# Attention on one Trainium2 core: mixing moved to four quadrants in the logits' banks, the final in its own bank, normalising over two rounds

## The reference

```
n = 56*56 tokens, 8 images, 8 heads of 16
q, k, v = x @ Wq.T, x @ Wk.T, 2 * (x @ Wv.T)       # [n, 8, 16]
v_h = v / |v|;  q = q / |q|;  k = k / |k|
A = softmax(v_h @ v_h.T)                            # 8 x 8 per token
q, k = A @ q, A @ k                                 # mixing over heads
P = softmax(k.T @ q)                                # 16 x 16 per token
out = v @ P                                         # 8 x 16 per token
out = transpose(out, (0, 3, 1, 2)).reshape(n, 128)  # per image, across tokens
return out @ proj_w.T + proj_b                      # added to x
```

## Time and profile before

| | |
|---|---|
| median of 3 runs | 3337.49 us (3333.54 to 3340.35) |
| the profiled execution | 3327.52 us, span 3325.7 us |
| PE busy | 2987.1 us (90%), 62,769 matmul and 62,769 load instructions |
| DVE busy | 1866.8 us (56%) |
| ACT busy | 1275.8 us (38%) |
| POOL busy | 570.3 us (17%) |

### The profile page before, as it was taken

The page is one execution under the profiler, slowest core; times in us unless marked ns, Lnnn a source line. Parts: engine busy times, 40 slices in busy tenths (PEclk is TensorE's granted clock), DMA queues, the critical chain, the costliest instruction groups (busy, mean ns, idle before and its releaser), DMA issues. The chain is left out here.

```text
span 3325.7 us, 143922 instructions
## 1 busy us (share of the span) xinstructions
PE 2987.1 (90%) x62769; PEld 2207.7 (66%) x62769; DVE 1866.8 (56%) x3334; ACT 1275.8 (38%) x2841; POOL 570.3 (17%) x419
## 2 busy tenths in 40 slices
PE   6686989999999999999998995889888898988897
PEld 5463369766666666666665443777777777777777
DVE  4452542566666666666665773555555555555553
ACT  3453552422222222222222443444444444444431
POOL 0000030022222222222221222111111111111111
PEclk8787889999999999999999996999999999999999
DMA  6877000021112121212114985555555555564551
GB/s 143 229 227 198 1 1 1 13 47 45 46 44 46 43 46 43 46 44 45 45 44 174 414 326 139 84 85 95 103 109 85 104 91 113 85 110 85 104 85 49
DMA packets 1015824, 318.88 MB, mean 96 GB/s; under 512 B 863345, under 2 KB 1002158, under 8 KB 1010350
## 3 DMA queue, kind: packets, MB, share of 16 engines
q1 hardware_dynamic: 692626, 169.81, 24.7%
q10 hardware_dynamic: 322844, 143.73, 15.8%
HBM read 157.66 MB, written 155.75 MB: 94 GB/s over the span
## 5 line engine op out<-in xcount | busy, mean ns | idle before, releaser
L845 DVE TENSOR_TENSOR terms<-spec,ps_z 112x456 f32<-112x456 f32 x1024 | 575.0, 623 | 404.4 <-PE ps_z L728 404.4
L738 PEld LDWEIGHTS ps_q<-inv_w,prod 112*57 112x57 f32 x16384 | 450.9, 133 | 174.6 <-issue 172.2
L738 PE MATMUL ps_q<-inv_w,prod 112*57 112x56 f32 x16384 | 484.4, 217 | 1.2 <-DVE prod L851 1.2
L826 POOL TENSOR_TENSOR prod<-terms 112x456 f32<-112x456 f32 x256 | 297.6, 1162 | 1000.6 <-DVE terms L845 1000.6
L728 PE MATMUL ps_z<-x_half,fwd_w 120*112 120x456 f32 x1024 | 458.4, 570 | 0.0
L783 ACT ACTIVATE q_half<-ps_q 121x448 f32<-121x448 f32 x255 | 138.9, 545 | 827.3 <-PE ps_y L746 827.3
L1131 POOL TENSOR_TENSOR k_blocks<-k_mixed,same_of 128x896 f32<-128x896 f32 x112 | 193.4, 1727 | 1071.2 <-ACT k_mixed L1274 1071.2
L1180 PE MATMUL ps_l<-q_mixed,k_blocks 32*64 32x64 f32 x12544 | 230.1, 220 | 66.4 <-issue 65.6
L1180 PEld LDWEIGHTS ps_l<-q_mixed,k_blocks 32*64 32x64 f32 x12544 | 205.3, 133 | 83.2 <-issue 75.2
L1157 PEld LDWEIGHTS ps_s<-v_blocks 128*64 128x64 f32 x6272 | 199.0, 141 | 90.0 <-issue 81.0
L728 PEld LDWEIGHTS ps_z<-x_half,fwd_w 120*112 120x112 f32 x1024 | 160.4, 176 | 121.9 <-issue 106.1
(11 more groups left out here) (140 smaller groups left out, 4340.0 us busy)
## 6 DMA issues: line engine op xcount, KB each, us to landing
qk_heads<-st_qk ACTq DMA_DIRECT2D x56, 476.0 KB, 4.6
qk_rows<-qk_heads SPq DMA_DIRECT2D x56, 476.0 KB, 6.8
conv_in<-v_sb ACTq DMA_DIRECT2D x112, 224.0 KB, 3.3
v_in<-conv_in SPq DMA_DIRECT2D x512, 49.0 KB
conv_out<-y_sb ACTq DMA_DIRECT2D x512, 49.0 KB
y<-conv_out SPq DMA_DIRECT2D x8, 1792.0 KB, 13.6
x_in<-in_x SPq DMA_DIRECT2D x8, 1568.0 KB, 9.5
shortcut<-short ACTq DMA_DIRECT2D x8, 1568.0 KB, 6.2
```

The lines of the kernel that those rows point to most:

```text
L738: last = pe.matmul(ps_q[64 * ri:64 * ri + NF, c * SIDE:(c + 1) * SIDE], prod[b % 2][:, x, c * NF:(c + 1) * NF], k.inv_w[:, x, ri * SIDE:(r ...
L826: pool.tensor_tensor(prod[b % 2][:, 1, :], terms[b % 2][:, 2, :], terms[b % 2][:, 3, :], ALU.add).then_inc(prod_i_r, 1)
L845: last = dve.tensor_tensor(terms[b % 2][:, x, :], k.spec[0:NFFT, s, bass.ds(c * CC, CC), :].rearrange("p c f -> p (c f)"), ps_z[b % 2][z][ ...
```

## The change

`mix` writes ps_l, the two banks of the logits, in the columns behind theirs (272 and up), and ps_mix goes. Even groups write bank 0, odd groups bank 1, and odd groups swap halves: rows a go to half a ^ (g % 2). What is read from the mixing keeps its place in each group, so from there on odd groups have their halves swapped; `outputs` undoes it by choosing v_blocks and the half of ps_o by r = a ^ (g % 2). `mix(i)` now waits for exp_l of unit i-2, and `logits(i-1)` for both readers of mix(i). The bank that ps_mix had goes to the second projection, and ps_f is the final's alone: two waits go. The rounds are reordered on PE, ACT and DVE, and `normalize` is cut in two halves in two rounds, with `store_heads` behind them.

```
-        ps_a, ps_m, ps_o, ps_f = (psum(n) for n in ("ps_qkv", "ps_mix", "ps_o", "ps_qkv_fin"))
+        ps_a, ps_b, ps_o, ps_f = (psum(n) for n in ("ps_qkv0", "ps_qkv1", "ps_o", "ps_fin"))
...
+    MC = (GU + 3) * HD
+    MW = GU // 2 * QKM
...
             def mix(i):
...
+                if i >= 2:
+                    pe.wait_ge(l_exp, i - 1)
                 for g, gb in groups(i):
                     for a in range(2):
                         rows = slice(64 * a, 64 * a + 64)
-                        last = pe.matmul(ps_m[rows, g * QKM:g * QKM + 64], eb[i % 2][rows, g, :], strided(qk[n % NIN][rows], gb * QKW, [[1, 64]]), start=True, stop=True)
+                        half, at = 64 * (a ^ g % 2), MC + g // 2 * QKM
+                        last = pe.matmul(ps_l[half:half + 64, g % 2, at:min(at + 64, 512)], eb[i % 2][rows, g, :], strided(qk[n % NIN][rows], gb * QKW, [[1, min(64, 512 - at)]]), start=True, stop=True)
...
             def logits(i):
-                pe.wait_ge(q_r, i + 1)
                 pe.wait_ge(k_r, i + 1)
+                pe.wait_ge(q_r, min(NU, i + 2))
+                pe.wait_ge(km_r, min(NU, i + 2))
...
             def outputs(i):
...
-                        last = pe.matmul(ps_o[64 * a:64 * a + 64, g * HD:g * HD + 64], vb[n % NIN][:, gb, a, :], pn[i % 2][:, a, g:g + 4, :], start=True, stop=True)
+                        r = a ^ g % 2
+                        last = pe.matmul(ps_o[64 * r:64 * r + 64, g * HD:g * HD + 64], vb[n % NIN][:, gb, r, :], pn[i % 2][:, a, g:g + 4, :],
+                                         start=True, stop=True)
...
             def final(b, u):
-                pe.wait_ge(qkv_read, min(NB * BPB, AHEAD * BPB + 2 * (b * UPI + UPI + 3 + u)))
...
                 if bk < NB * BPB:
                     project(bk)
-                    if i in FINS:
-                        b, u = FINS[i]
-                        pe.wait_ge(f_r, b * 8 + u + 1)
                     project(bk + 1)
...
             def leave_mix(i):
-                ps = ps_m[:, 0:GU * QKM].rearrange("p (g x) -> p g x", x=QKM)
+                ps = ps_l[:, :, MC:MC + MW].rearrange("p j (g x) -> p g j x", x=QKM)
...
-                if i % 2 == 1 and i // 2 + AHEAD - 1 < NB:
-                    store_heads(i // 2 + AHEAD - 1)
-                if unit(i):
-                    leave_mix(i)
+                if i % 2 == 0 and i and i // 2 + AHEAD - 2 < NB:
+                    store_heads(i // 2 + AHEAD - 2)
...
-            def normalize(n):
+            def normalize_q(n):
...
+            def normalize_kv(n):
+                a = n % 2
+                scale_rows(n, 1, HD + 1)
```

More of the change, by code:

```diff
@@ L1140, in project @@
                     pe.wait_ge(qkv_read, bk - 1)
-                pe.matmul((ps_f if bk % 2 else ps_a)[0:TB, 0:3 * CH], xn[n % 3][:, j * TB:(j + 1) * TB], k.w[:, WQ:WQ + 3, :].rearrange("p a c -> p (a c)"),
+                pe.matmul((ps_b if bk % 2 else ps_a)[0:TB, 0:3 * CH], xn[n % 3][:, j * TB:(j + 1) * TB], k.w[:, WQ:WQ + 3, :].rearrange("p a c -> p (a c)"),
                           start=True, stop=True).then_inc(qkv_ps, 1)
@@ L1213, in _ @@
                 bk = AHEAD * BPB + 2 * i
+                if unit(i):
+                    mix(i)
                 if unit(i + 1):
@@ L1239, in copy_in @@
                     act.wait_ge(st_r, n - 1)
-                to, ps = sq[bk // 2 % 2][:, j % 2], (ps_f if bk % 2 else ps_a)[0:TB, 0:3 * CH]
+                to, ps = sq[bk // 2 % 2][:, j % 2], (ps_b if bk % 2 else ps_a)[0:TB, 0:3 * CH]
                 act.activation(to[:, 0:2 * CH], ps[:, 0:2 * CH], ACT.Square)
@@ L1272, in leave_mix @@
                     act.wait_ge(k_r, i - 1)
-                act.activation(dsq[i % 2][:], ps[:, :, HD:HD + 1], ACT.Square).then_inc(d_r, 1)
-                act.activation(km[i % 2][:], ps[:, :, HD + 1:], ACT.Copy).then_inc(km_r, 1)
+                act.activation(dsq[i % 2][:].rearrange("p (g j) x -> p g j x", j=2), ps[:, :, :, HD:HD + 1], ACT.Square).then_inc(d_r, 1)
+                act.activation(km[i % 2][:].rearrange("p (g j) x -> p g j x", j=2), ps[:, :, :, HD + 1:], ACT.Copy).then_inc(km_r, 1)
             def store(b, u):
@@ L1296, in _ @@
                     root(i // 2 + AHEAD - 1)
+                if unit(i):
+                    leave_mix(i)
                 if unit(i + 1):
                     exp_s(i + 1)
-                if i % 2 == 1 and i // 2 + AHEAD - 1 < NB:
-                    store_heads(i // 2 + AHEAD - 1)
-                if unit(i):
-                    leave_mix(i)
+                if i % 2 == 0 and i and i // 2 + AHEAD - 2 < NB:
+                    store_heads(i // 2 + AHEAD - 2)
                 if unit(i - 1):
@@ L1322, in clamp, with scale_rows @@
                 dve.tensor_scalar(nsc[n % 2][:], nsq[n % 2][:], 1e-24, None, ALU.max).then_inc(nsc_r, 1)
-            def normalize(n):
+            def scale_rows(n, x, at):
+                a = n % 2
+                dve.tensor_tensor(st_qk[a][:, :, :, at:at + HD], qkv[a][:, :, x * CH:(x + 1) * CH].rearrange("p j (h d) -> p j h d", d=HD),
+                                  bcast(rn[a][:, :, 8 * x:8 * x + 8], 3, HD), ALU.mult)
+            def normalize_q(n):
                 a = n % 2
@@ L1331, in normalize @@
                 dve.wait_ge(rn_r, n + 1)
-                for x, at in ((0, 0), (1, HD + 1)):
-                    dve.tensor_tensor(st_qk[a][:, :, :, at:at + HD], qkv[a][:, :, x * CH:(x + 1) * CH].rearrange("p j (h d) -> p j h d", d=HD),
-                                      bcast(rn[a][:, :, 8 * x:8 * x + 8], 3, HD), ALU.mult)
+                scale_rows(n, 0, 0)
+            def normalize_kv(n):
+                a = n % 2
+                scale_rows(n, 1, HD + 1)
                 dve.tensor_tensor(st_v[a][:].rearrange("p j (d h) -> p j d h", h=HEADS), qkv[a][:, :, 2 * CH:].rearrange("p j (d h) -> p j d h", h=HEADS),
@@ L1352, in weigh @@
                     dve.wait_ge(l_ps, i - 1)
-                dve.tensor_tensor(qm[a][:, 0:GU, :], ps[:, :, 0:HD], wgt[a][:].to_broadcast([128, GU, HD]), ALU.mult).then_inc(q_r, 1)
+                dve.tensor_tensor(qm[a][:, 0:GU, :].rearrange("p (g j) d -> p g j d", j=2), ps[:, :, :, 0:HD],
+                                  wgt[a][:].rearrange("p (g j) x -> p g j x", j=2).to_broadcast([128, GU // 2, 2, HD]), ALU.mult).then_inc(q_r, 1)
             def divide(i):
@@ L1390, in _ @@
                     if pr // 2:
-                        normalize(pr // 2 - 1)
+                        normalize_q(pr // 2 - 1)
+                        normalize_kv(pr // 2 - 1)
             mask(0)
             for i in range(ROUNDS):
+                if unit(i):
+                    weigh(i)
                 if unit(i + 1):
@@ L1397, in _ @@
                     leave(i - 2)
-                if unit(i):
-                    weigh(i)
+                if i // 2 + AHEAD - 1 < NB:
+                    (normalize_kv if i % 2 else normalize_q)(i // 2 + AHEAD - 1)
                 if unit(i - 1):
@@ L1408, in _ @@
                         clamp(pr // 2)
-                if i % 2 == 0 and i // 2 + AHEAD - 1 < NB:
-                    normalize(i // 2 + AHEAD - 1)
 def build(nc, t):
```

1 line of the change is left out of this document (removed).

## The result

The changed kernel takes 3310.52 us, the median of 4 runs (3308.4 to 3312.36), against 3335.51 us for the kernel before (3332.25 to 3340.35, 4 runs). The ratio is 0.993, with a 95% interval from 0.9909 to 0.9951. It is faster by 25 us. The forecast was a saving of 50 us: the direction holds, the size is off by half.

The account below looks back on a forecast made before the run. Bounds: TensorE's own work and, at two fifths of packets, late instructions. Of 95 + 22 = 117 us cut, 68 survive late packets; less 5, 6 and 7, 50 saved: 3287.5 us, own range 3257 to 3307, overall 3225 to 3345.

Parts of the forecast that it names:

- Part (1): Mixing on four quadrants: 56 records in 0.93 us, 0.85 us less per round, 95 us over 112 rounds.
- Part (2): Outputs with halves in the order 0, 1, 1, 0: cost taken as 0, bounds 0 and 0.8 us a round.
- Part (3): Final in its own bank: project no longer waits for its eviction, 0.37 us in 56 rounds, 22 us.
- Part (4): Mixing in the logits' banks, with new waits and order: 0.1 to 0.3 us lost per pair without a final, up to 7.
- Part (5): Normalising over two rounds, heads stored one round later: same work, mostly hidden, at worst 1 us in each of 24 pairs.
- At the 42% that are late the shortening is lost: TensorE is first at 107 of 256 instruction packets, so of 117 us only 117 x 0.58 = 68 is kept.
- 5 and 6 us: Further packet losses: 5 us for 23 more packets made late, 6 for unlisted short waits and busier DMA engines.
- The 7 us for late chains: Deduction for the chains of parts (4) and (5) running late in pairs of rounds without a final: 7 us.
- The first rival: Packet requests follow TensorE's place in the program, so nearly all 117 us is kept: 3227 to 3245 us; chance 0.17.
- mixing keeps 32 ns: Rival: mixing's pace per record stays, only the final's wait goes: 3329 us; chance 0.09.
- The engines behind hold TensorE: Rival: weigh late in even rounds or heads landing late under load: 3332 us, or 3320 for less; chance 0.09.
- the array overlaps only neighbours: Rival: mixing gains 0 and outputs lose 0.8 us in each of 112 rounds: 3376 us; chance 0.07.

Follow-up runs that it names:

- a_alt: The changed kernel with only the order of the outputs' halves put back to 0, 1, 0, 1: 3307.76 us.
- a_shared: The changed kernel with the final back in the second projection's bank and its two waits back: 3377.95 us.
- a_order: The changed kernel with mixing and outputs on two quadrants, the final in the second projection's bank and the normalising whole; reordering and shared mixing/logits banks stay: 3412.53 us.
- a_norm: The changed kernel with a block's normalising whole at the end of an even round and the heads' store where it was before: 3365.63 us.
- b_norm: The kernel before with only the normalising spread over two rounds and the store one round later: 3362.45 us.

## Why the prediction was half right

- Part (1), mixing at 0.93 us from the four quadrants of ps_x: 0.96 measured, 92 us and not 95. The Trainium skill, TensorE: Matmul & The Clock Gate, Part 3: Packing small matmuls, has loads overlap only across row groups, and by that alone mixing would have gained nothing. Its row groups alternate as before and it takes 0.96 us for 1.78, so row groups alone do not set the pace here, and the measurement decides.
- Part (2), the outputs' order at 0: right (a_alt).
- Part (3), the final's wait at 22 us: 22 by the records. But that is its price in the kernel before. In the kernel after, with the normalising spread, a_shared shows 67.
- Part (4), the logits' wait for the readers of mixing: in the layout it had half a microsecond to spare in even rounds, and in the kernel after there is no such wait. Right, and narrower than it sounds: a_order shows the other side of the same wait, 55 us, and a_norm 42.
- Part (5), the spreading at about 0: wrong as a price of its own. It is worth 55 us in the kernel after (a_norm) and costs 29 in the kernel before (b_norm). Parts (3), (4) and (5) were costed as separate terms and hold each other up. In the sum this did no harm, because all were made together.
- The step that failed is the sum. Of its terms, 117 us of work removed is right (114). "At the 42% that are late the shortening is lost", with its 5 and 6 us, took 60 us for the packets; 70 were measured. The 42% come from the list of waits, which leaves out short ones: by gaps over 0.15 us, 131 of 254 boundaries were late before, 52%, and 164 after, 65%. The mean of the two, 0.58 x 114 = 66, comes near. It is a rough rule: for the pair with fewer instructions it gives 46, where 37 were measured, for the pair without the reads 45, where it was 62. The larger miss is a term that the sum put at nothing: longer waits bring the half clock, 51 us more of it in the traces, at most 25 us, and 19 by what the rest leaves of the measured gain. The 7 us for late chains were not seen. With the bound, 114 - 70 - 25, the forecast would have been 19. No run changes the clock alone, so its share rests on this balance.
- The first rival (packets cost less) is dead: the gaps grew. That mixing keeps 32 ns is dead. "The engines behind hold TensorE" did not happen in this kernel, but a_norm is that rival to the letter, at 3366 and not 3332. That the array overlaps only neighbours is dead too: the outputs take 1.63 us as before.

## What to carry to other kernels

When a straight list of instructions feeds a busy TensorE, look at the queue of instructions before pricing a cut: count the boundaries at which it is dry by gaps, short ones too, and expect that share of the cut to be lost, or more, since the cut makes others late (52% before and 65% after here, that is 59 and 74 us of 114, where 70 were lost). Add what the clock does behind each long wait. Fewer instructions for the same columns, or less traffic on the other queues, moved the time more here (113 and 100 us in the kernel before, in experiments that leave work out) than the 114 us cut from the instructions' own time (25 us).

Price the parts of a change together where one makes the wait that another covers. And when a row says "issue", see whether the start follows the end of a producer by the same short time round after round, 0.1 us in the 50 rounds here, and whether the program waits for it there: then it is a wait for that producer.

## What was not expected of the hardware

A packet of instructions is used about 2.5 us after its start in all traces here, and starts 1.16 to 2.15 us (means) after TensorE crosses the boundary before it, depending on the other queues. Moving the same reads or stores of the heads in time did not change this mean; leaving out 567,000 packets, nearly all under 512 bytes, did, by 0.56 us (after) and 0.68 (before). Behind the load of x for an image, 1568 KB in packets of 12,544 bytes, the start came 3.54 us after the boundary on average. A wait of 3.44 us was followed by 6.82 us at half clock. Why the amount of the heads' traffic matters and its moment does not is open.
